# One attention and feed-forward block on one core: the loop over seven key chunks written out with constant semaphore counts

## The reference

```python
q = (M @ Wq.T).reshape(e, h, dh).transpose(1, 0, 2)      # M: 512 x 512
kv = x @ Wkv.T + bkv                                     # x: 6250 x 256
k, v = jnp.split(kv, 2, axis=-1)                         # 8 heads of 64
sim = jnp.einsum('hid,hjd->hij', q, k) * dh ** (-0.5)
sim = jnp.where(mask, sim, -1000000000.0)
attn = jax.nn.softmax(sim, axis=-1)
out = jnp.einsum('hij,hjd->hid', attn, v)
out = out.transpose(1, 0, 2).reshape(e, h * dh) @ Wo.T + bo
m = layer_norm(out + M)
ffn = jax.nn.relu(m @ W1.T + b1) @ W2.T + b2             # W1: 2048 x 512
z = layer_norm(ffn + m)
```

## Time and profile before

| what | value |
|---|---|
| median of 3 runs | 700.93 us (700.62 to 702.13) |
| the profiled execution, its own time | 701.8 us |
| its span | 700.0 us, 11125 instructions |
| TensorE (PE) busy | 633.1 us, 90% |
| VectorE (DVE) busy | 552.6 us, 79% |
| ScalarE (ACT) busy | 364.3 us, 52% |
| GpSimd (POOL) busy | 246.0 us, 35% |
| mean granted TensorE clock | 0.977 of full |

### The profile page before, as it was taken

One profiled execution on the slowest core, in us unless ns is written; L12 is line 12 of the kernel. 1 busy time (PEld: TensorE's weight loads), 2 busy tenths in 40 slices (PEclk: granted clock), 3 DMA queues, 4 the chain that ended last, 5 costly groups with the idle time before them and its releaser, 6 DMA issues.

```text
span 700.0 us, 11125 instructions
## 1 busy us (share of the span) xinstructions
PE 633.1 (90%) x3382; PEld 397.7 (57%) x3382; DVE 552.6 (79%) x688; ACT 364.3 (52%) x658; POOL 246.0 (35%) x305
## 2 busy tenths in 40 slices
PE   3967999999999999998999999999999697999994
PEld 2655555554565555555655556655555344688883
DVE  5378899989999999997998999899999835333334
ACT  5355655565656555664555565556556413333332
POOL 2212453236322642264223632263222404422223
PEclk9998999999999999999999999999999899799998
DMA  8037798988888889888888888888887982133211
GB/s 285 1 78 203 202 220 207 250 210 200 215 242 200 216 212 231 224 200 201 204 227 202 209 220 246 199 197 216 204 202 179 253 234 93 31 97 104 99 60 60
DMA packets 54938, 128.37 MB, mean 183 GB/s; under 512 B 15840, under 2 KB 19424, under 8 KB 54624
## 3 DMA queue, kind: packets, MB, share of 16 engines
q1 hardware_dynamic: 44128, 101.97, 56.3%
q10 hardware_dynamic: 10752, 25.70, 14.3%
HBM read 23.80 MB, written 1.05 MB: 35 GB/s over the span
## 4 chain that ended last, share of the span: by engine, by line
PE 57%; DVE 18%; issue 8%; SPq 7%; DMA 4%; ACT 3%; ACTq 2%; DVEq 1%; POOL 1%; POOLq 0%
PE tail L855 14%; PE slot L827 12%; DVE st L681 8%; PE tail L752 8%; PE slot L752 7%; PE slot L906 6%; SPq L350 6%; PE slot L914 6%; DVE prob L671 5%; DMA pt<-st 2%; PE tail L862 2%; ACT prob L533 2%; ACTq L569 2%; DMA wq_raw<-in_wq 1%; PE slot L786 1%
## 5 line engine op out<-in xcount | busy, mean ns | idle before, releaser
L533 ACT ACTIVATE prob<-prob,negmax 128x896 f32<-128x896 f32 x224 | 233.8, 1044 | 213.0 <-DVE negmax L671 195.9
L671 DVE CUSTOM_DVE_ANT_0 prob<-slot,lower,negmax_old 128x896 f32<-128x896 f32 x224 | 249.0, 1149 | 42.1 <-PE slot L827 30.0
L681 DVE STREAM_TRANSPOSE st<-prob 128x1792 f32<-128x1792 f32 x112 | 228.6, 2041 | 3.5 <-DMA pt<-st 3.2
L855 PE MATMUL tail<-pt,val 128*64 128x512 f32 x784 | 185.2, 607 | 7.1 <-ACT outT_sb L553 5.7
L827 PE MATMUL slot<-k_hi,q_hi 64*128 64x448 f32 x448 | 95.3, 416 | 18.7 <-DVE negmax L671 15.3
L855 PEld LDWEIGHTS tail<-pt,val 128*64 128x64 f32 x784 | 51.5, 138 | 103.0 <-issue 94.6
L827 PEld LDWEIGHTS slot<-k_hi,q_hi 64*128 64x128 f32 x448 | 43.9, 184 | 86.3 <-issue 76.9
L827 PE MATMUL slot<-k_hi,q_lo 64*128 64x448 f32 x448 | 84.3, 364 | 0.0
L827 PE MATMUL slot<-k_lo,q_hi 64*128 64x448 f32 x448 | 84.1, 363 | 0.0
L430 POOL TENSOR_TENSOR total<-total,alpha 128x8 f32<-128x8 f32 x28 | 5.8, 207 | 196.8 <-ACT alpha L573 196.8
L443 POOL TENSOR_TENSOR k_lo<-k_raw,k_hi 128x896 fp32r<-128x896 f32 x27 | 57.1, 2115 | 3.9 <-POOL k_hi L440 0.2
(11 more groups left out here) (112 smaller groups left out, 814.2 us busy)
## 6 DMA issues: line engine op xcount, KB each, us to landing
pt<-st SPq DMA_DIRECT2D x672, 112.0 KB, 3.0
pt<-st ACTq DMA_DIRECT2D x224, 112.0 KB, 3.3
w_raw<-in_w SPq DMA_DIRECT2D x32, 256.0 KB, 2.8
x_raw<-in_x SPq DMA_DIRECT2D x13, 448.0 KB, 4.0
mask_raw<-in_mask SPq DMA_DIRECT2D x7, 448.0 KB, 4.7
mt_raw<-in_mt SPq DMA_DIRECT2D x2, 512.0 KB, 8.2
wq_raw<-in_wq SPq DMA_DIRECT2D x2, 512.0 KB, 8.7
wo_raw<-in_wo SPq DMA_DIRECT2D x1, 1024.0 KB, 6.6
```

The lines of the kernel that those rows point to most:

```text
L533: nc.scalar.activation(unit, unit, ACT.Exp, bias=negmax[:, p, u:u + 1], scale=-1.0, accum_out=psumrow[:, p, u:u + 1]).then_inc(exp_done, 1)
L671: nc.vector.tensor_tensor_reduce(out=prob[:, i % 2, h].rearrange("p (b n) -> p b n", b=2), in0=slot[:, j, :, :HALF], in1=lower[:, i].rearr ...
L681: nc.vector.transpose(st[:, g].rearrange("p b k (t i) -> p k b t i", t=2)[:, :, :, t2], prob[:, i % 2].rearrange("p h (k b i) -> p (h k) b ...
L855: last = nc.tensor.matmul(outT[DH * h:DH * h + DH], val[:, val_at(i, parity ^ (p < 0)), head(p, h)], moving, start=(i == 0), stop=(i == KT ...
```

## The change

All seven chunks are called with a number for `c`. Each engine's program then holds seven bodies one behind another in place of five, the counts are constants within the waits, and the register of the loop, its arithmetic and its branch are gone. The steps, their order, their buffers and what waits for what are the same.

```diff
         def chunks(eng, body):
-            body(0, chunk_schedule(True, False), 0)
-            mid = chunk_schedule(False, False)
-            body(1, mid, 1)
-            with eng.Fori(2, CHUNKS - 2, 2) as c:
-                body(c, mid, 0)
-                body(c + 1, mid, 1)
-            body(CHUNKS - 1, chunk_schedule(False, True), 0)
+            for c in range(CHUNKS):
+                body(c, chunk_schedule(c == 0, c == CHUNKS - 1), c % 2)
```

## The result

| | median, 21 runs | profiled execution | its span |
|---|---|---|---|
| before | 702.27 us (700.45 to 706.4) | 701.8 us | 700.0 us |
| after | 698.78 us (696.85 to 702.62) | 698.3 us | 696.5 us |

The ratio is 0.9947, 95% interval 0.9934 to 0.996: faster by 2.8 to 4.6 us. The three runs of before that stood ahead of the prediction had a median of 700.93; with 18 more it is 702.27.

A forecast was written before the change was run, and what follows sets the result against it. TensorE and VectorE, both nearly full in each chunk, were taken to bound the kernel. Branch stall 2.82 us plus its aftermath 0.41 gave 3.22 (rounded), so 700.93 - 3.22 = 697.7 us, range 696.2 to 699.8.

The forecast's parts named there:

- The taken branch goes: End of chunk 3: removing the loop's taken branch and its instruction-fetch stalls gains 2.82 us, bounds 2.24 to 3.0.
- The two losses are parallel and of one size, so both must go for the gain to come: At the taken branch: TensorE alone loses about 3.0 us, VectorE 2.8, and the change takes both away.
- ScalarE's slack covers it: At the taken branch: ScalarE idles 6.80 us, some 4 above its usual wait, but is not late for the next transpose.
- What the stall leaves behind: Chunk 4: engines leave the stall out of step; at 74.44 us instead of 74.85 it gains 0.41, bounds 0 to 0.58.
- Register instructions, 0: Chunks 2 to 5: removing register instructions gains 0; bounds -0.33 us a chunk to +5.3 if VectorE's lay on the path.
- Rival A: Chunks 4 and 5: straight code arrives late, about 2.82 us a block; one block 4%, two or more 4%.
- Rival C: Feed-forward start, granted clock 0.76: the shift may cost TensorE 2.0 us more, giving 699.7 us; 7%.
- Rival D: Gap at 328 us: branch is cheap, about 108 ns, and something else causes the gap; time 700.8 us, 1%.

The follow-up runs named there:

- the short loop: Changed kernel, but VectorE alone loops, over one chunk in four passes; chunks 3 and 4 together took 149.28 us, against 148.85 written out.
- the six: The six kernels without a two-chunk loop on TensorE or VectorE, the changed kernel included; chunks 3 and 4 together took 148.85 to 149.67 us, mean 149.2.
- the feed-forward run: Changed kernel with the feed-forward's loops written out too, on all engines; ratio to before 0.9924 (0.9899 to 0.9949).
- the loops of one pass: Kernel before with its loop over chunks 2 to 5 split into two loops of a single pass each, on all engines; ratio to before 0.9943.
- TensorE's second run: Second look at the kernel with the loop kept on TensorE alone, other engines written out; chunks 3 and 4 together took 152.56 us.
- the first run: First look at the kernel with the loop kept on TensorE alone, other engines written out; chunks 3 and 4 together took 151.53 us.

## Why the prediction was right, and where it was not

The forecast was a gain of 3.22 us. The medians differ by 3.49 (702.27 - 698.78), and the ratio gives 3.7 with an interval of 2.8 to 4.6. The median after, 698.78, is 1.1 above the 697.7 forecast, within the range; the base more than makes up for that, three runs at 700.93 where 21 give 702.27.

- *The taken branch goes, 2.82 us*: right in mechanism and size. Chunk 3 lost 77.27 - 74.45 = 2.82; that it is the same to the hundredth is luck, since without a long branch on TensorE or VectorE chunk 3 took 74.37 to 74.74. That it is the branch is shown by its place, by TensorE's 4.285 us taken against 0.083 not taken, by the code packets, and on VectorE by the short loop. No run has all the register instructions and no taken branch; the chunks without one, 2 and 5, bound what they can add.
- *"The two losses are parallel and of one size, so both must go for the gain to come"*: wrong. Parallel they mostly are, of one size they are not. TensorE's alone is worth 2.7 us, and 3.7 where the clock fell with it; VectorE's is 0.8 to 1.0, or 0.4 to 0.7 over the mean of the six. Writing out TensorE and leaving VectorE and ScalarE in the loop already wins 1.7. The prediction took VectorE's 2.24 us of idleness and the 2.8 by which its chunk was long as VectorE's own price. Part of it came of the branch being reached late: in the kernel before the last transpose waits 0.63 us for a DMA, with VectorE's sequencer held in front of the branch.
- *ScalarE's slack covers it*: right. 5.1 us of standing still moved nothing. (The 6.80 us were some 5 above the 1.64 of the same place after the change, not 4.)
- *What the stall leaves behind, 0.41 us*: not shown. The sum over chunks 2 to 5 did fall by 3.43, so the total agrees, and that is in part luck: a run with no stall had the same long chunk 4 (74.89), and long chunks turn up at other places too (75.90 us in the short-loop run's chunk 5, 76.02 and 75.30 in chunks 1 and 4 of the feed-forward run). In each of these one transpose waits for a DMA, 1.55, 1.66 and 1.26 us. The kernel before has such a wait, of 0.62 us, in its chunk 4, 26 us behind the stall (its line is below). The 0.41 is within that scatter, and that the engines left the stall out of step is not shown.
- *Register instructions, 0*: right, by chunks 2 and 5 of the kernel before and by each kernel with one engine looped. The bound of +5.3 us was too low: it counts line 239 alone, and VectorE's register instructions of chunks 2 to 5 come to 8.7 us.
- *Rival A, a late block in straight code*: not seen in the written-out kernel; no gap with "issue" stands at the boundary of chunks 3 and 4, and no chunk from 1 to 5 is over 74.8 us.
- *Rival C, the clock*: the start of the feed-forward is granted 0.80 over 17 us where it had 0.76. The tail from chunk 6 on takes 217.1 us against 217.8, and 215.7 to 218.3 over the other kernels, so the 0.7 is within chance. The clock did play a part that the prediction did not foresee, at the branch itself (below).
- *Rival D, the bare price of a branch*: ruled out by TensorE's 4.285 us against 0.083 in one kernel.

The row of the changed kernel for that clock:

```profile
592.00:609.00 17.00, 15.14 (x56) 11.53 (x57) 6.65 (x10) 6.10 (x11) 8.83 (x8) 0.80 0.11 32
```

The line of the kernel before in its chunk 4:

```profile
358.38 2.04 DVE L681 STREAM_TRANSPOSE st<-prob 128x1792 f32<-128x1792 f32 x1 [0.62 <-DMA pt<-st]
```

## What to carry to other kernels

Look for the taken branch of a long loop on each engine's sequencer and compare the time to the next instruction with that of the same branch when it is not taken: here 4.4 against 0.08 us on TensorE, and 3.7 us on VectorE where its idleness shows 2.2. Ask which engine's stall the others wait for, by looping one engine at a time; the engine with the largest visible gap need not be the one that pays, and the idle time of an engine whose neighbour stalls too is not its own price. Register counts in waits cost nothing measurable here, so where a loop is wanted a shorter body may do as well as constants; this was shown on VectorE only. And look at the trace of an experiment for the instructions that it is meant to keep: the loops of one pass had lost theirs.

## What the runs showed of the hardware

- The stall on TensorE can bring the clock down behind it. In two of the four profiles with a looped TensorE the granted clock fell to 1.2 GHz for 3.3 us or a little more right after the stall (0.50 over 328.7 to 332.0 us in the row of TensorE's second run); in the kernel before and the first run it stayed at 1.00. The second run took 1.0 us more than the first. In none of the thirteen profiles did the clock fall anywhere else in chunks 1 to 5, but two cases are few, and what decides between a fall and none is open.
- A taken branch on VectorE takes its sequencer 0.3 to 0.4 us over one chunk of code and 3.1 to 3.8 us over two; on ScalarE over two it takes 3.5 to 4.2, on TensorE 4.3 to 4.7; on GpSimd and SyncE, with two chunks, 0.3 to 0.4. Other engines' stalls seem to lengthen it: VectorE's took 3.1 to 3.2 us in the three profiles in which TensorE did not loop and 3.7 and 3.8 in the two in which it did, ScalarE's 3.5 in two and 4.2 in one. Why is open. A shorter loop on TensorE was not tried. The Trainium skill, "Runtime: NRT & Kernel Launch", section "Instruction fetch mechanics", names the cause, a target outside a small window of code. The runs agree with it, by the short loop and by the packets (q14: 29 with VectorE's long loop, 22 with the short one, 25 with none), and do not measure the window.
- In all four kernels with a looped TensorE the last transpose of chunk 3 waited 0.22 to 0.77 us for a DMA, at 327.8 to 328.7 us, and in none of the others. A 16 KB packet of code on q8 had started some 3 us earlier in each (at 324.8 to 325.8 us). That the fetch delays the data's DMAs is a guess that no run tested.
